# A graph kernel's first layer: 288 instead of 272 edge tiles counted in groups, over 62 instead of 64 steps of uneven windows

## What is computed

```python
# layer 0
summed = segment_sum(x[src], dst, n)          # 100000 gathered rows of 256
deg    = segment_sum(ones, dst, n)
out    = concatenate([x, summed / max(deg, 1)], -1) @ weight
out    = out / norm(out) + bias
# layer 1
h = feats * rsqrt(deg_out)[:, None]
m = segment_sum(h[src], dst, n) * rsqrt(deg_in)[:, None]
x = m @ W_gc + b_gc + feats @ W_res + b_res
y = x + top2_mixture_of_64_experts(x)          # then a norm over columns
```

## Time and profile before

| | us |
|---|---|
| median of 3 runs | 2180.07 |
| lowest, highest | 2176.84, 2180.3 |
| the profiled execution | 2177.57 |
| its span in the trace | 2175.8 |
| layer 0's steps in it | 48.2 to 693.2 |
| layer 1's steps in it | about 794 to 1431 |

### The profile page before, as it was taken

One profiled execution on the slowest core, in us unless ns is written; L12 is line 12 of the kernel. 1 busy time (PEld: TensorE's weight loads), 2 busy tenths in 40 slices (PEclk: granted clock), 3 DMA queues, 4 the chain that ended last, 5 costly groups with the idle time before them and its releaser, 6 DMA issues.

```text
span 2175.8 us, 49992 instructions
## 1 busy us (share of the span) xinstructions
PE 1846.2 (85%) x14730; PEld 1499.6 (69%) x14730; DVE 1211.4 (56%) x3624; ACT 808.5 (37%) x2522; POOL 1316.5 (61%) x1383
## 2 busy tenths in 40 slices
PE   2899999999976738999999999777539999999757
PEld 1588888888863515888888888556427788777535
DVE  5978888888843864545555554236713333333395
ACT  3656556555522632222222222033422222222137
POOL 3677777777775727777777777727744444444300
PEclk9999999999996969999999999878769999999959
DMA  5444544444345043343443344623148866476763
GB/s 187 136 143 141 148 141 141 146 143 141 110 134 170 0 145 116 113 115 112 117 113 114 112 115 116 223 63 49 38 106 263 261 192 189 142 240 190 233 195 119
DMA packets 218664, 308.55 MB, mean 142 GB/s; under 512 B 46930, under 2 KB 164745, under 8 KB 218492
## 3 DMA queue, kind: packets, MB, share of 16 engines
q0 software_dynamic: 60112, 151.05, 24.4%
q1 hardware_dynamic: 103388, 101.82, 15.0%
q10 hardware_dynamic: 54992, 53.49, 7.8%
HBM read 293.77 MB, written 57.83 MB: 162 GB/s over the span
## 4 chain that ended last, share of the span: by engine, by line
PE 58%; DMA 10%; DVE 10%; issue 7%; POOL 7%; ACT 4%; SPq 1%; DVEq 1%; POOLq 0%; another core or an unknown queue 0%; ACTq 0%
PE bank L1144 21%; DMA acc<-x_scratch,acc 6%; POOL gath L717 6%; PE bank L1181 5%; PE bank L1353 4%; PE bank L1111 4%; PE bank L1344 4%; PE bank L1163 4%; PE bank L1167 4%; PE bank L1096 3%; PE bank L1242 3%; ACT past_hi L846 2%; DVE Y L1969 2%; DMA gath<-h_scratch,idx_t 1%; DMA gath<-in_x_dram,idx_t 1%
## 5 line engine op out<-in xcount | busy, mean ns | idle before, releaser
L717 POOL DMA_INDIRECT gath<-in_x_dram,idx_t x512 | 496.9, 971 | 187.4 <-issue 145.1
L717 POOL DMA_INDIRECT gath<-h_scratch,idx_t x480 | 475.7, 991 | 186.8 <-issue 136.2
L1144 PE MATMUL bank<-Y,X 128*128 128x128 f32 x4704 | 580.0, 276 | 0.0
L1144 PEld LDWEIGHTS bank<-Y,X 128*128 128x128 f32 x4704 | 563.6, 192 | 18.7 <-issue 2.5
L863 ACT ACTIVATE Y<-bank 128x400 f32<-128x400 f32 (+1 forms) x384 | 170.0, 494 | 427.7 <-PE bank L1167 427.7
L1541 DVE TENSOR_TENSOR oh_lo<-bank,lohi_t 128x512 bf16<-128x512 f32 x392 | 265.5, 680 | 0.2 <-DVE flag_s L1513 0.2
L1574 DVE TENSOR_TENSOR acc<-acc,bank 128x256 f32 x248 | 104.5, 421 | 277.9 <-issue 260.6
L846 ACT ACTIVATE past_hi<-iota_code,below_hi 128x50 bf16<-128x50 f16 x784 | 198.5, 325 | 123.0 <-PE bank L1127 113.1
L999 ACT ACTIVATE acc<-bank,acc 128x128 f32<-128x128 f32 x388 | 111.6, 368 | 326.4 <-PE bank L1344 284.7
L1096 PE MATMUL bank<-gath,sums_work 128*32 128x256 f32 x1984 | 186.2, 397 | 53.5 <-DMA gath<-h_scratch,idx_t 30.9
L808 POOL DMA_INDIRECT y_scratch<-acc x96 | 97.6, 1017 | 210.3 <-DVE acc L1946 204.2
(11 more groups left out here) (260 smaller groups left out, 2679.6 us busy)
## 6 DMA issues: line engine op xcount, KB each, us to landing
acc<-in_L_gnn_w_dram SPq DMA_DIRECT2D x101, 512.0 KB
acc<-in_L_gnn_w_dram ACTq DMA_DIRECT2D x96, 512.0 KB
y_scratch<-bias_s ACTq DMA_DIRECT2D x49, 256.0 KB
y_scratch<-bias_s SPq DMA_DIRECT2D x98, 128.0 KB
Y<-y_scratch SPq DMA_DIRECT2D x14, 896.0 KB, 13.1
acc<-in_L_gnn_b_dram ACTq DMA_DIRECT2D x96, 128.0 KB
gath<-in_x_dram,idx_t POOLq DMA_INDIRECT x512
gath<-h_scratch,idx_t POOLq DMA_INDIRECT x480
```

What stands on the lines that cost most here:

```text
L717: pool.indirect_dma_start(out=gath[:, half, k, :], out_offset=None, in_=table, in_offset=bass.IndirectOffsetOnAxis(ap=idx_t[:, TD[L] + t:T ...
L1144: last = pe.matmul(DB[w % 2][:, c * P:(c + 1) * P], X[:, h, c * P:(c + 1) * P], panel[:, w % 2, h, :], start=(L == 1 and h == 0), stop=(h ...
```

## The change

Layer 0 gets 12 groups: nine of (1, 1, 6) and three of (0, 4, 4), each of 6 units, 72 units or 288 tiles. 496 tiles are gathered over 62 steps. The one window length per layer gives way to a table of lengths: 4, then 5 and 4 in turn six times, then 4. The units of the 12 groups lie in windows 0 to 11 (steps 0 to 53), the slices in windows 1 to 12 (steps 4 to 57), the last panels in window 13. A window of 4 steps with 6 units has two of them in its first and in its third step. Layer 1's table is fifteen fours, which is what it had. `window_of` finds the window of a step; the waits are the same ones, counted by window.

```diff
-GROUP_PANELS = (((1, 1, 6),) * 7 + ((1, 3, 4),) * 2 + ((0, 4, 4),) * 2,
+GROUP_PANELS = (((1, 1, 6),) * 9 + ((0, 4, 4),) * 3,
                 ((1, 1, 6),) * 9 + ((0, 2, 6), (0, 4, 4)) * 2)
-WINDOW = (5, 4)
+LENGTHS = ((4,) + (5, 4) * 6 + (4,), (4,) * 15)
...
-        W = WINDOW[L]
+        begin = [sum(LENGTHS[L][:w]) for w in range(ND[L] + 2)]
         at = [[] for _ in range(ST[L])]
         slices = [(0, 0, 0)] * ST[L]
         for w, units in enumerate(groups[L]):
             for u, unit in enumerate(units):
-                at[W * w + u * W // len(units)].append((w,) + unit)
-            for k in range(W):
-                slices[W * (w + 1) + k] = (w, SLICES * k // W, SLICES * (k + 1) // W)
+                at[begin[w] + u * LENGTHS[L][w] // len(units)].append((w,) + unit)
+            n = LENGTHS[L][w + 1]
+            for k in range(n):
+                slices[begin[w + 1] + k] = (w, SLICES * k // n, SLICES * (k + 1) // n)
...
+    def window_of(L, st):
+
+        w = max(w for w, begin in enumerate(begins[L]) if begin <= st)
+        return w, st - begins[L][w]
+
     def panel_adds(L, st):
 
-        w, k = st // WINDOW[L] - 2, st % WINDOW[L]
+        w, k = window_of(L, st)
+        w -= 2
...
-                b, k = e % TABS, (st // WINDOW[0] + 1) % 2
-                opens = st % WINDOW[0] == 0 and e == hist_first[st]
-                if opens and st >= 3 * WINDOW[0]:
-                    pe.wait_ge(acc_step, acc_dense[0][st // WINDOW[0] - 3])
+                w, since = window_of(0, st)
+                b, k = e % TABS, (w + 1) % 2
+                opens = since == 0 and e == hist_first[st]
+                if opens and w >= 3:
+                    pe.wait_ge(acc_step, acc_dense[0][w - 3])
```

More of the change, by code:

```diff
@@ L119, in gnn_kernel @@
     for L in range(2):
-        assert ST[L] * GROUP + TD[L] == ET and WINDOW[L] * (ND[L] + 1) < ST[L] and NT <= ST[L] and ST[L] % 2 == 0
+        assert ST[L] * GROUP + TD[L] == ET and len(LENGTHS[L]) == ND[L] + 2 and sum(LENGTHS[L]) == ST[L] and NT <= ST[L] and ST[L] % 2 == 0
     QROW0 = TE // QUAD
@@ L126, in gnn_kernel @@
     SLICES = DC * NT
-    units_at, slices_at, first_unit, first_panel, panels_by = [], [], [], [], []
+    begins, units_at, slices_at, first_unit, first_panel, panels_by = [], [], [], [], [], []
     for L in range(2):
-        W = WINDOW[L]
+        begin = [sum(LENGTHS[L][:w]) for w in range(ND[L] + 2)]
         at = [[] for _ in range(ST[L])]
@@ L135, in gnn_kernel @@
             for u, unit in enumerate(units):
-                at[W * w + u * W // len(units)].append((w,) + unit)
-            for k in range(W):
-                slices[W * (w + 1) + k] = (w, SLICES * k // W, SLICES * (k + 1) // W)
+                at[begin[w] + u * LENGTHS[L][w] // len(units)].append((w,) + unit)
+            n = LENGTHS[L][w + 1]
+            for k in range(n):
+                slices[begin[w + 1] + k] = (w, SLICES * k // n, SLICES * (k + 1) // n)
+        begins.append(begin)
         units_at.append(at)
@@ L164, in gnn_kernel @@
             a += len(panel_adds(L, st))
-            if len(acc_dense[L]) == st // WINDOW[L] - 2 and st % WINDOW[L] == PANELS // ADDS - 1:
+            if window_of(L, st) == (len(acc_dense[L]) + 2, PANELS // ADDS - 1):
                 acc_dense[L].append(a)
@@ L1594, in add_degrees @@
                 dve.wait_ge(hist_done, hist_first[st] if st < ST[0] else HU)
-                hist = HISTB[-(-st // WINDOW[0]) % 2]
-                if st == WINDOW[0]:
+                hist = HISTB[(window_of(0, st - 1)[0] + 1) % 2]
+                if st == begins[0][1]:
                     return v.tensor_copy(deg_raw, hist)
@@ L1600, in add_panels @@
             def add_panels(L, st):
-                if L == 0 and st % WINDOW[0] == 0 and st > 0:
+                if L == 0 and st in begins[0][1:]:
                     add_degrees(st)
```

## The result

| | before | after |
|---|---|---|
| median of 5 runs | 2180.07 | 2196.03 |
| lowest, highest | 2175.22, 2180.99 | 2192.99, 2200.86 |
| the profiled execution's span | 2175.8 | 2194.3 |
| last sums of layer 0 | 693.2 | 707.0 |
| from there to the end of the span | 1482.6 | 1487.3 |

The ratio is 1.0078, with a 95% interval of 1.0063 to 1.0093. The change makes the kernel 16 us slower, 0.8%; 2190 in all was forecast, from 11 us more in layer 0. Of the 18.5 us by which the two spans differ, 13.8 lie in layer 0 and 4.7 behind it, where both kernels run the same code.

The account below looks back on a forecast made before the run. Layer 0 was taken as DVE-bound in the head, PE-bound with POOL level in the middle, POOL-bound in the tail. Head 85.5, windows 254.5 and 5 x 47.6, step 49 and tail gave 704.4, +11.2 us: 2190, range 2181 to 2199.

Parts of the forecast that it names:

- Three regimes: Layer 0: head paced by DVE, middle by PE with POOL level, tail by POOL.
- middle by PE with POOL level: Kernel before, layer 0's middle: PE busy 50.0 of 51.0 us a window; POOL needs 50.4 for 40 gathers.
- a microsecond taken from POOL counts in the tail only: Layer 0: POOL savings count only in the tail; time added to PE counts wherever POOL is not already behind.
- Windows of 4: Layer 0, windows 2, 4, 6, 8, 10: PE-paced, 47.6 us each, bounds 46.3 and 48.5.
- the bound from layer 1's window: Windows of 4: layer 1's 42.5 us plus 3.8 for 14 degree quads gives 46.3, before waits for DVE.
- Windows of 5: Layer 0, windows 1, 3, 5, 7, 9: unchanged at 50.9 us each, 254.5 in all.
- The head: Layer 0's window 0, paced by DVE: second unit in step 2 adds 2.9 us; ends at 85.5, bounds 81.6 and 87.
- step 49: Last step slower than POOL's 10.1 us: takes 11.5, ends at 589.5, with 409 gathers issued.
- The tail: Layer 0 behind step 49: POOL paces 87 gathers left, 114.9 us, end 704.4; last group's slices hidden.
- The reload of Y: Layer 0's tail: begins behind the last slices, five steps before the end as before, so it hides again.
- Moves as a block: Work behind layer 0 shifts by the same 11 us; over 3 us of change there would show the forecast wrong.
- the likely case: PE-bound middle and POOL-bound tail, 75%: 2184.5 to 2198, from bounds of head and windows and 2.5 for runs.

Follow-up runs that it names:

- short ends: Changed kernel's 12 groups and 62 steps with layer 0 lengths 3, eleven of 5, 2, 2, and four panel adds a step; 2177.88, ratio 0.9991.
- ends and cover: Lengths 3, eleven of 5, 2, 2, plus nine slices between two units and the previous step's shift ahead of slices in unit-less steps; 2180.01, ratio 0.998.
- cut in 11: Changed kernel with 96 of the 98 slices of layer 0's last group, 11 (steps 54 to 57), left out; 2197.04, ratio 1.0065.
- changed, cut in 5: Changed kernel with 96 of the 98 slices of layer 0's group 5 (window 6, steps 27 to 30) left out; 2185.54, ratio 1.004.
- before, cut in 5: Kernel before with 96 of the 98 slices of group 5 (steps 30 to 34) left out; 2182.3, ratio 1.0009.
- fives first: Changed kernel with layer 0's window lengths reordered: 4, then six of 5, then seven of 4; 2195.27, ratio 1.0084.
- four versions: Kernel before with first-window units 1, 1, 1, 1, 2; changed kernel with nine slices between units; short ends with cover; changed kernel without group 11's slices; 1.001 to 1.0044.

## Why the prediction was right, point by point

**Three regimes.** For the changed kernel they held, and the cuts show two of them: a window of 4 without its slices gave 10.0 us back, the same cut in the tail nothing. The head was not tested by a run of its own on a chip of the usual pace. For the kernel before, the prediction's "middle by PE with POOL level" doesn't hold as it stands: the same cut gave 0.8 us, and POOL never pauses, so the pace there is POOL's with PE level. So its "a microsecond taken from POOL counts in the tail only" was wrong as well: the count of POOL's time shows it. From its 17th gather to its last it takes 628.7 us before and 643.5 after. Sixteen gathers fewer take off some 21 us, wherever they stood, and the 35.6 us of pauses put more back: 25 of them lie in the short windows of PE, which last longer than 32 gathers do, and most of the rest in the step right behind one. With a 17th gather that leaves 0.7 earlier, the last one leaves 14.1 later. The forecast's sum didn't suffer from this, since it priced every window of the changed kernel by PE. That PE's own pace in a window of 5 is the same 50.9 us is seen where POOL has 7 to 9 gathers in front:

```profile
186.10:237.00 50.90, 50.03 (x522) 42.58 (x522) 40.62 (x105) 29.36 (x112) 37.38 (x39) 1.00 0.48 138
```

**Windows of 4.** Forecast 47.6, measured 47.7. The parts fit too: the first step 12.5, the third 13.3, with the wait in the third of 0.9 (1.0 forecast). POOL got ahead until its buffer was full, and waits of a gather for PE's sums of up to 3.4 us appeared (4.8 in the window); in the kernel before none is longer than the cadence's 0.3. In all PE wasn't busy for 1.25 us of the window (47.70 less 46.45), which is the 1.3 that was put on top of the bound from layer 1's window.

**Windows of 5.** Mis-sized by 1.2 us in sum, half of it in the first one: 51.5 instead of 50.9, the other four 50.9 to 51.2. Its first step took 12.3 (86.9 to 99.2) where the first steps of the other long windows take 11.8 to 12.0, and DVE was busy for 11.95 of it (9.56 in the row of before), which fits a DVE that came out of the short head behind. The 50.9 was carried over unchanged, and that was the error.

**The head.** The largest miss of the layer: it ended at 86.9, forecast 85.5 (bound 87). Steps 2 and 3 took 22.2 us, forecast 20.1. Step 2 alone took 16.0, not 11.6. The forecast had priced the second unit by DVE's own 2.9 us. In the head no slices cover it, and PE waits both for its one-hots and for ACT's copies, from 58 to 88 us:

```profile
PE bank L1172 <- DVE oh_lo L1550: 3.4, 2, 1.8
PE bank L1172 <- ACT Y L871: 2.1, 3, 0.7
```

And in the second part of the step PE's granted clock stood at 0.50, 1.2 instead of 2.4 GHz:

```profile
64.70:73.80 9.10, 4.46 (x36) 2.88 (x36) 8.04 (x20) 5.99 (x24) 6.97 (x8) 1.00 0.50 145
73.80:80.60 6.80, 5.90 (x42) 2.74 (x42) 6.66 (x17) 3.94 (x16) 4.12 (x5) 0.50 0.35 99
```

Ahead of the fall PE was busy for 4.46 of 9.10 us; behind it 42 matmuls hold it for 5.90 us, where 36 took 4.46. DVE is busy all the while (6.66 of 6.80), so no run here says what the clock alone cost. The head's 1.4 us and the long windows' 1.2, less 0.2 in the short ones, are the 2.4 us by which step 48 ended late (580.4, forecast 578.0), and nearly all of the 2.6 us by which step 49 (592.1, forecast 589.5) and the layer did (707.0, forecast 704.4).

**The tail.** Exact: 409 gathers issued at its start and 114.9 us. But its waits have changed. The weight loads wait 11.9 us for gathers, where it was 34.3, and PE waits 12.3 us for one-hots, where it was 2.4:

```profile
PE bank L1136 <- DVE oh_lo L1550: 12.3, 8, 2.7
...
PEld bank L1104 <- DMA gath<-in_x_dram,idx_t: 11.9, 14, 1.5
```

These cost nothing, as the cut in the tail shows: behind step 49 POOL never pauses, and what PE waits for doesn't matter as long as gathers leave every 1.259 us. The reload of Y hid, as forecast, since it was over before the last gathers left: the end came 5.3 us after the start of the last gather (701.73), against 5.6.

```profile
701.73 0.95 POOL L725 DMA_INDIRECT gath<-in_x_dram,idx_t  x1 [0.30 <-issue]
```

**Behind the layer.** This step failed. "Moves as a block" was put at zero, with more than 3 us named as a sign that something was wrong; it was 4.7 us in the spans and 2.2 in the medians (16.0 less 13.8). By stages, the two traces differ so:

| | before | changed |
|---|---|---|
| last sums of layer 0 to first sums of layer 1 | 113.9 | 116.0 |
| sums of layer 1 | 624.3 | 623.7 |
| from there to the experts' loop | 179.6 | 182.5 |
| experts' loop | 444.2 | 444.9 |
| the rest | 120.6 | 120.2 |

Over the eight kernels the first of these falls into two kinds. It is 116.0 to 116.4 us in the changed kernel, with short ends, with ends and cover and with the cut in 11, and 113.8 to 114.3 in the other four. In exactly the first four the granted clock falls to 0.50 for 3.4 us, some 32 us behind layer 0's last sums. The row of the changed kernel, then the same place in the kernel before:

```profile
739.40:742.80 3.40, 3.40 (x8) 2.75 (x9) 2.24 (x6) 2.35 (x8) 0.09 (x1) 0.51 0.00 0
```

```profile
725.60:729.00 3.40, 2.54 (x11) 1.58 (x9) 3.40 (x8) 2.30 (x8) 2.26 (x4) 1.00 0.01 2
```

In the 17 us before that fall PE was busy for 14.2. Why the clock falls in four of the kernels and not in the others is open, and so is whether it does so in every run of a kernel. The 2.9 us in front of the experts' loop have no such mark; that stage takes 178.4 to 184.5 us over the eight. From the layer's last sums to the end of the span:

| before | changed | changed, cut in 5 | before, cut in 5 | fives first | short ends | ends and cover | cut in 11 |
|---|---|---|---|---|---|---|---|
| 1482.6 | 1487.3 | 1483.9 | 1489.5 | 1492.6 | 1494.7 | 1495.8 | 1491.3 |

The code is the same in all eight (in the seventh the slices' order differs in layer 0 only), and the stretch varies by 13.2 us. Between the kernel before and the one with short ends most of it is in the experts' loop, 444.2 us against 454.8 (one row of each; for the changed kernel the loop explains only 0.7 of its 4.7):

```profile
1611.00:2055.20 444.20, 411.56 (x2612) 342.60 (x2611) 140.68 (x678) 112.84 (x389) 190.39 (x192) 0.99 0.69 211
```

```profile
1604.40:2059.20 454.80, 414.49 (x2611) 346.10 (x2611) 140.36 (x678) 112.74 (x389) 190.37 (x192) 0.98 0.66 207
```

The engines' busy times agree within 4 us; the rest is waiting. The kernel before is the shortest of the eight. In the medians, too, the part that layer 0 doesn't explain is never below zero: 3.2 with the cut, 5.5 for the kernel before with it, 9.4 with fives first, 7.1 and 3.8 for the two versions with short ends, 0.2 for the cut in the tail. One trace for each kernel can't say whether that is chance or whether the stage depends on when, or in what state, layer 0 leaves it. That stays open. It is where the layer's gain of 6.5 us with fives first is lost, and it is a term of 0 to 9 us that a forecast of this kernel should have carried as a range.

**How much was luck.** The layer's 13.8 us alone put the kernel at 2193.9, inside the range. The term behind it happened to be 2.2 us; with the 9.4 of fives first the time would have been 2203, outside it. And the lower end of the likely case, 2184.5, is not what its listed bounds give: 4 and 6.5 us below 2190, with 2.5 for the runs, are 2177.

## What to carry to other kernels

Added and removed work of equal sums doesn't cancel. Here two engines were level, POOL without a pause and PE 1 us short of full in 51. Taking 20 us from POOL and giving 21 us to PE made POOL stand for 36 us, and the layer longer by 14. To tell which of two busy engines sets the end, look for pauses in the cadence of each and cut one's work in a single place. Put the added work where another engine sets the pace (here the tail, at no cost), and look what is beside it: a short end brought a reload onto the last gathers and a pause in front of them, and gave back 5 of the 13 us that were forecast for it. When a stage far behind the change varies by more than the change does, read the stage of the change in the trace, and carry the rest as a range.

## What the runs showed of the hardware that wasn't expected

On two of the chips every kernel took about 2820 and 2870 us instead of 2180, with ACT and DVE standing still for 7 to 10 us about once a step and PE's weight loads for up to 6.6. The ratios of four versions to the kernel before lie between 1.001 and 1.0044 there, so they say little about a chip of the usual pace.

A gather beside other traffic keeps its cadence of issue (0.95 us and 0.30) but not its time under way: 7.64 and 7.98 us for the last one with the DMA share at 1.04 and 1.01, against 4.21 and 4.42 where the reload was over by then.

The same program text ran for 2 us longer in one stage in four of eight kernels, each time with 3.4 us at a granted clock of 0.50 in the middle of a stretch where the others have 1.00.
